# A fused Perceiver block on one core: scores of the next pair issued before the weighted sum, both row maxima behind them, and the context rows copied by VectorE

## What is computed

```python
def xattn(Q, K):                       # 16 heads, latents of width 32
    C_q, C_kv = Q @ Wq_d, K @ Wkv_d    # 512 -> 64, 512 -> 32
    CqWqk = (C_q @ W_qk).reshape(b, n, 16, 32)
    scores = einsum('bnhl,bkl->bhnk', CqWqk, C_kv) / sqrt(32)
    V_up = (C_kv @ Wv_u).reshape(b, nkv, 16, 32)
    return einsum('bhnk,bkhd->bnhd', softmax(scores), V_up)
x = x + xattn(layernorm(x), ctx)
x = x + attn(layernorm(x))             # one head of 128, Wqkv, bias, Wo, bias
xh = layernorm(x) @ hadamard           # then 4-bit codes per row, ternary weight
x = x + (codes(xh) @ ternary(weight).T)
```

## Time and profile before

| | us |
|---|---|
| time, median of 3 runs | 314.23 (314.06 to 314.25) |
| the profiled execution's own time | 315.06 |
| its span, first to last instruction | 313.3 |

### The profile page before, as it was taken

How to read it: one execution, slowest core, us unless ns; L and a number is a source line. 1 busy time by engine, 2 the same in 40 slices (tenths; PEclk the granted TensorE clock), 3 DMA queues, 4 the chain that set the end, 5 groups by cost and what they waited for, 6 DMA issues and landing times.

```text
span 313.3 us, 8324 instructions
## 1 busy us (share of the span) xinstructions
PE 299.5 (96%) x3043; PEld 207.5 (66%) x3058; DVE 246.9 (79%) x530; ACT 208.1 (66%) x587; POOL 90.0 (29%) x130
## 2 busy tenths in 40 slices
PE   7997989999999999999999999999999999999993
PEld 6754857667576766768576766768576866648642
DVE  1689798887879878887879878887879878896366
ACT  2578478768596676768596676768596777784400
POOL 2008304140323324051323324051323324141411
PEclk9999799999999999999999999999999999999998
DMA  7995002051311603041310603051311102000001
GB/s 216 376 363 187 4 8 96 19 189 31 106 49 36 186 1 134 17 157 61 108 43 33 184 0 134 17 173 44 110 43 63 26 0 69 19 35 2 33 0 67
DMA packets 20968, 26.94 MB, mean 86 GB/s; under 512 B 10704, under 2 KB 11472, under 8 KB 20944
## 3 DMA queue, kind: packets, MB, share of 16 engines
q1 hardware_dynamic: 20944, 26.62, 26.1%
HBM read 20.71 MB, written 4.19 MB: 80 GB/s over the span
## 4 chain that ended last, share of the span: by engine, by line
PE 74%; DVE 11%; ACT 6%; DMA 3%; SPq 2%; issue 2%; POOL 0%; DVEq 0%; POOLq 0%
PE ps L1009 10%; PE ps L1074 9%; PE ps L957 7%; PE ps L1132 5%; PE ps L1112 4%; PE ps L1078 4%; PE ps L1162 4%; ACT prob L385 4%; PE ps L967 3%; PE ps L1185 3%; PE ps L1156 3%; DMA bo_row<-bo 3%; PE ps L1046 3%; PE ps L1030 2%; DVE mx L614 2%
## 5 line engine op out<-in xcount | busy, mean ns | idle before, releaser
L385 ACT ACTIVATE prob<-ps,nmx,qk_scale 128x128 f32<-128x128 f32 x240 | 89.8, 469 | 34.9 <-DVE nmx L618 34.9
L1009 PE MATMUL ps<-had_s,x3t 128*128 128x512 f32 x104 | 48.2, 605 | 0.7 <-ACT x3t L379 0.7
L614 DVE TENSOR_REDUCE mx<-ps 128x8 f32<-128x1024 f32 x31 | 37.7, 1217 | 7.0 <-PE ps L1132 7.0
L334 POOL TENSOR_TENSOR qk_scale<-aux,power 128x1 f32<-128x1 f32 x16 | 9.3, 580 | 98.4 <-DVE aux L636 98.4
L623 DVE TENSOR_REDUCE sum_a<-prob 128x8 f32<-128x1024 f32 x30 | 35.8, 1210 | 0.0
L379 ACT ACTIVATE prob_t<-ps 128x512 f32<-128x512 f32 x63 | 34.8, 622 | 0.7 <-PE ps L957 0.3
L1009 PEld LDWEIGHTS ps<-had_s,x3t 128*128 128x128 f32 x104 | 18.6, 190 | 24.5 <-issue 22.7
L957 PE MATMUL ps<-ident,prob 128*128 128x128 f32 x240 | 31.8, 276 | 2.1 <-ACT prob L385 2.1
L957 PEld LDWEIGHTS ps<-ident,prob 128*128 128x128 f32 x240 | 26.6, 141 | 5.5 <-ACT prob L385 4.7
L1074 PE MATMUL ps<-x2t,wqkv_s 128*128 128x128 f32 x224 | 28.6, 281 | 0.4
L1074 PEld LDWEIGHTS ps<-x2t,wqkv_s 128*128 128x128 f32 x224 | 26.1, 192 | 2.2 <-ACT x2t L379 1.3
(11 more groups left out here) (200 smaller groups left out, 577.1 us busy)
## 6 DMA issues: line engine op xcount, KB each, us to landing
ct<-ctx_cols SPq DMA_DIRECT2D x16, 512.0 KB, 4.8
xt<-x_cols SPq DMA_DIRECT2D x16, 256.0 KB, 2.9
xr<-x_rows SPq DMA_DIRECT2D x16, 256.0 KB, 4.2
y<-res SPq DMA_DIRECT2D x15, 256.0 KB, 2.0
had_s<-hadamard SPq DMA_DIRECT2D x1, 1024.0 KB, 7.7
w_rows<-weight SPq DMA_DIRECT2D x1, 1024.0 KB, 10.7
wqkv_s<-wqkv SPq DMA_DIRECT2D x1, 768.0 KB, 8.4
wqk<-w_qk SPq DMA_DIRECT2D x2, 128.0 KB, 4.3
```

The lines of the kernel that those rows point to most:

```text
L385: last = nc.scalar.activation(prob[:, h, :], ps[:, h // 4, (h % 4) * P:(h % 4) * P + P], ACT.Exp, bias=nmx[:, h:h + 1], scale=qk_scale[:])
L614: V.tensor_reduce(mx[:, h], ps[:, 2 * half:2 * half + 2, :].rearrange("p r (c k) -> p (r c) k", c=EC), AX.X, ALU.max).then_inc(done["mx"], 1)
L1009: mm = pe.matmul(ps[:, B4, :], x3t[:, c, :], had_s[:, c, :], start=(c == 0), stop=(c == EC - 1))
```

## The change

From round 2 on (`scores_first`), and with line numbers of the kernel before:

- TensorE: `projected` (L1030) goes ahead of the second attention's scores (L1097) and now also waits for `read["qk"]`. The scores (L1132) go ahead of L1142, and the weighted sum (L1112) behind it.
- The copy of the context rows goes from ScalarE to VectorE (`context`), ahead of the second attention's maximum (L644).
- VectorE: in odd rounds the row statistics (L628 to L636) go ahead of the query copy (L640). The maximum over banks 2 and 3 leaves the next round's place behind the `x2` statistics and stands right behind the one over banks 0 and 1, ahead of `prod` (L769) and `x3` (L776). The tail loses its copy of it (L859, L862).

```diff
+        def scores_first(i, par):
+            return not (isinstance(i, int) and i <= 1)
...
# ScalarE
-                if front and not (isinstance(i, int) and i == 0):
+                if front and not scores_first(i, par) and not (isinstance(i, int) and i == 0):
                     after(act, made["ckv"], i + 1)
                     copy(ckv[:, 1 - par], ps[:, B1, 0:2 * SKV]).then_inc(read["ckv"], 1)
...
# VectorE
+                def context():
+                    after(dve, made["ckv"], i + 1)
+                    V.tensor_copy(ckv[:, 1 - par], ps[:, B1, 0:2 * SKV]).then_inc(read["ckv"], 1)
...
-                if cross and not (first and i == 1):
+                if cross and first and (i == 0 or i == 2):
                     largest(i, 1)
...
+                if front and scores_first(i, par) and par == 1:
+                    row_variance()
+                    row_scale()
                 if front and par == 1 and not alone(i) and not (first and i == 1):
                     second_query()
+                if front and scores_first(i, par):
+                    context()
                 if self_ and not (first and i == 1):
                     second_max()
                 if cross and par == 0 and not (first and i == 0):
                     sums(1)
-                if front and not (first and 0 <= i <= 1):
+                if front and not (scores_first(i, par) and par == 1) and not (first and 0 <= i <= 1):
                     row_variance()
                     row_scale()
...
                     largest(i + 1, 0)
+                    if scores_first(i, par):
+                        largest(i + 1, 1)
...
-            V.tensor_reduce(mx[:, 8:16], ps[:, 2:4, :].rearrange("p r (c k) -> p (r c) k", c=EC), AX.X, ALU.max)\
-                .then_inc(done["mx"], 1)
-            dve.wait_ge(done["mx"], N * 2 + 2)
-            V.tensor_scalar(nmx[:, 8:16], mx[:, 8:16], qk_scale[:], -1.0, ALU.mult, ALU.mult).then_inc(done["nmx"], 1)
...
# TensorE
+                if front and scores_first(i, par):
+                    after(pe, read["qk"], i - 1)
+                    after(pe, read["lat"], i + 1)
+                    projected()
...
-                if front and not (first and i == 0):
+                if front and not scores_first(i, par) and not (first and i == 0):
                     projected()
...
-                if cross:
+                if cross and not scores_first(i, par):
                     weighted_sum()
+                if front and scores_first(i, par):
+                    scores()
                 if self_:
                     after(pe, done["exp2"], i - 1, 2)
                     pe.transpose(ps[:, B3, 0:P], p2[:], ident[:]).then_inc(made["p2t"], 1)
-                if front and not (first and i == 0):
+                if cross and scores_first(i, par):
+                    weighted_sum()
+                if front and not scores_first(i, par) and not (first and i == 0):
                     scores()
```

## The result

The change makes the kernel slower: **328.07 us** (327.81 to 329.24, 4 runs) against 314.24 (314.06 to 315.74, 4 runs), a ratio of 1.0444 with a 95% interval of 1.0423 to 1.0465, or +13.8 us. The profiled execution took 328.21 us, its span is 326.4 us.

A forecast was written before the change was run, and what follows sets the result against it. TensorE, busy 96%, was taken as the bound, with VectorE's x3 just in time. Six even and six odd rounds, 6 x (1.82 + 0.56) = 14.3, plus 2.1 for round 14, gave +16.4 us: 330.6 us, range 326 to 336.

The forecast's parts named there:

- x3 had next to no slack: At the end of round 8, VectorE's x3 comes just in time: it ends at 168.87 and TensorE needs it at 168.97.
- the second maximum: On VectorE ahead of prod and x3, it costs the same 1.39 us again as the first maximum with its negative.
- Even rounds: VectorE's list sets the end, with the x3 transposes 7.98 us behind the context rows: +1.82 us a round.
- Round 14: Same distance to the x3 transposes as round 8 but no gain at the x2t copy: +2.1 us.
- Odd rounds: VectorE sets the end at 6.49 us behind the context rows against TensorE's own 6.32: +0.56 us a round.
- The earlier `x2t` copy: In even rounds, ScalarE's earlier copy ends TensorE's 0.27 us wait ahead of L1074, of which 0.25 us is gained.
- TensorE hardly stands still: In round 8's 5.64 us from the weighted sum to the x3 transposes, TensorE was said to have almost no idle time.
- The sum: Six even and six odd rounds cost 14.3 us; with round 14 and the tail, +16.4 us together.
- Scores issued early bring nothing by themselves: In even rounds the scores end long before VectorE turns to them at 3.64 us, so issuing them early brings nothing.
- TensorE's clock: Rival: the granted clock falls in the new gaps, 1.7 us lost in every even round, +12 us, 342 us; chance 0.11.
- Faster: Rival: the x3 transposes don't wait for x3, VectorE having over 1.8 us to spare: 312.5 us; chance 0.03.
- refunded: Rival: TensorE runs ahead elsewhere and takes up x3's lateness, leaving 314 to 320 us; chance 0.06.

The follow-up runs named there:

- e1: The changed kernel with the second maximum put back behind the x2 statistics of the next round, and in the tail: 319.21 us, ratio 1.0128 to the kernel before.
- e3: The kernel before with only the second maximum moved, so that both maxima stand behind the scores: 328.50 us, ratio 1.0438.
- e5: The changed kernel with even rounds laid out as odd ones, second row sums and row statistics ahead of VectorE's context copy: 321.40 us, ratio 1.0195.
- e4: The kernel before with TensorE's new order alone, ScalarE making the context copy ahead of the two exponentials: 318.09 us, ratio 1.0094.
- e8: e5 with context matmuls between two sets of transposes and, in even rounds, row statistics behind the second attention's maximum: 321.06 us, ratio 1.0186.
- e2: The changed kernel with the context copy given back to ScalarE, ahead of its two exponentials of the second attention: 328.92 us, ratio 1.0458.
- e9: e6 with, in even rounds, ScalarE also copying query and key ahead of the second copy of probabilities: 314.62 us, ratio 0.9979.
- e6: The kernel before with, in even rounds, two instead of three exponentials of the second half ahead of the x2t copy: 313.81 us, ratio 0.9978.
- e7: The changed kernel with the second maximum moved behind x3, still in the same round: 326.02 us, ratio 1.0365.

## Why the prediction was right, and where its sizes were off

The sign, the mechanism and the place in even rounds were as forecast: 330.6 was forecast, +16.4 us, and 328.07 came, +13.8. The odd rounds came out near by their number, but what sets their end was taken wrongly. Point by point:

- **x3 had next to no slack, and the second maximum is what it waits for in even rounds.** Shown by e1 and e3, and by the wait of 1.32 us ahead of L983. The second maximum took 1.39 us of VectorE's list (172.76 - 171.37), the forecast term to the digit; taking it out in e1 gave 1.22 us back in the round. "No slack" was a little too strong: before, `x3` started 0.83 us behind `prod`, where 0.66 is enough in the changed kernel, and TensorE, not VectorE's list, held it back, so the list had 0.17 us to spare.
- **Even rounds: +1.82 forecast, +1.69 measured** in rounds 6 to 10. The term was 0.13 too large. L983 starts 7.89 us behind the context matmuls where 7.98 was worked out: the maximum follows the copy's start by 0.34 instead of 0.44, and `x3` follows `prod` by 0.66 instead of 0.74, against 0.13 more between that maximum and the first row maximum (3.28 instead of 3.15). In rounds 2 and 4 the excess was 1.36 and 1.55 only. Round 14 gave 2.04, forecast 2.1.
- **Odd rounds: +0.56 forecast, +0.29 to +0.40 measured**, and this is the step that failed in its reasons. I had VectorE set the end, at 6.49 behind the context matmuls against 6.32 for TensorE. L983 of round 7 starts at 6.39. In the trace `x3` ends at 157.17, TensorE's L978 at 157.27, and L983 follows it without a wait. TensorE's own order sets the end there and in rounds 5, 9 and 11; in rounds 3 and 13 L983 does wait, 0.17 and 0.18 us, for `x3`. TensorE waited longer ahead of the scores than I took: from the copy's end (151.27) to the scores 0.29 us pass, where I had 0.06; and from the scores' start to L983 5.66 us pass, where I had 5.80. The two errors work against each other, so that the odd term came out near is in part luck.
- **The earlier `x2t` copy: 0.25 us forecast, 0.14 measured.** L1085 starts 6.26 us behind the start of round 8, and L1074 before 6.40 us. The rest is lost because the transposes of `x2n` start 0.13 us later there (4.90 us instead of 4.77).
- **A wait of before was inside a number.** The chain gives L1030 0.63 us before, yet 0.45 after. The two matmuls are the same. Before, the weight loads of the weighted sum behind them waited for the last probability copy, in 13 rounds:

```profile
PEld ps L1112 <- ACT prob_t L379: 4.7, 13, 0.7
```

I read the difference as this wait, which the chain counted into L1030; that is argued from the order, and no run tests it. By it "TensorE hardly stands still" was too strong by 0.1 to 0.2 us a round. What the trace does show is that the context matmuls of the changed kernel ended earlier than I had them (10.51 us behind the start of round 8, where 10.59 was worked out).
- **The sum.** Rounds 2 to 13 were to cost 14.3 us and cost 11.7; round 14 and the tail were to cost 2.1 and cost 2.0. Of the 2.6 us, 0.7 lie in rounds 2 and 4. The 0.83 us that was added between the median and the profiled execution did not come back: the profile before had a granted clock of 0.79 from 28 to 36 us, the one after 1.00, and it lies 0.14 us above its median.
- **Scores issued early bring nothing by themselves** was said of even rounds and was right there (they end long before VectorE turns to them). It doesn't hold for odd ones: e3 shows that without them VectorE waits 0.77 us.
- **TensorE's clock** (rival): the page's row of the granted clock stays at 9 through all slices, and the mean is 1.000 in this execution. Gaps of up to 1.5 us in the rounds and one of 1.82 us at the head of the tail were not followed by a lower clock. The three executions that were not profiled have means of 0.996, 0.997 and 0.991, and the last took 329.24 us; where they lost it isn't known, but no such loss comes near the 12 us of this rival. **Faster** and **refunded** fell too: work that came early only waited elsewhere, as the table of waits shows.

## What to carry to other kernels

When one engine is nearly always busy, ending another engine's wait that isn't on the chain need not bring anything (here 26 us of ScalarE's waiting for the maxima went and 13.8 us were lost). Before moving a step on an in-order engine, look at what is listed behind it and how much slack that has: ahead of `x3`, which was done only 0.1 us before TensorE was free for its reader, the maximum took 1.39 us of VectorE's list and 1.2 us of an even round, and in e5, with other work moved into VectorE's idle stretch, it stands in the same place and the matmuls of round 8 have no marked wait for `x3` any more. And where a matmul, the copy of its result and the matmul that uses it follow each other, TensorE needs other work in between. Taking that work away exposed the context copy (0.50 us in e4), and shifting the first matmul forward exposed the next copy (0.42 us in e8).

## What the runs showed beside that

**The same gap, with and without a lower clock.** In round 1 the order of the instructions is the same in all these kernels, and TensorE waits there for ScalarE. In e4 and e2 the windows around this gap read (busy us of the engines, then granted clock, DMA share, GB/s; e4 first):

```profile
28.00:36.00 8.00, 5.93 (x44) 5.17 (x43) 7.72 (x15) 5.87 (x14) 5.46 (x6) 0.79 0.48 163
```

```profile
28.00:36.00 8.00, 5.86 (x55) 5.10 (x54) 7.72 (x15) 6.07 (x16) 5.63 (x6) 1.00 0.43 159
```

Both had a gap of 2.07 to 2.08 us just before 31 us, with TensorE busy 5.9 of 8 us; the mean clock fell to 0.79 in one, with 0.50 in the 2 us from 32 to 34 (1.2 GHz), and stayed at 1.00 in the other. Over the eleven profiled executions: seven had the gap of 2.07 to 2.08 us, and the clock of this stretch fell in five of them (before, e1, e4, e5, e9) and not in two (e2, e8). Four had a shorter gap there, 1.47 to 1.64 us (changed, e3, e6, e7), and it fell in none.

Of the 17 runs of the kernel before that were taken beside e5 to e7, the eight with a mean clock of 0.996 or more took 313.43 to 314.25 us, the eight with 0.991 or 0.992 took 315.14 to 316.02, and one with 0.657 took 418.51. 1.3 us between the medians of the two eights is more than e6 gains; with like clocks e6 stands at 313.46 against 314.13 and at 314.98 against 315.43. But the mean clock doesn't tell all: of the 17 runs beside e8 and e9, three with 0.999 or 1.000 took 315.3 to 315.4 us and one with 0.992 took 314.31. What decides whether the clock falls these runs don't tell.

**A scaled negative beside GpSimd.** The 128x8 step behind a maximum takes 0.23 us at the round's end. In the old place of the second maximum it overlaps with GpSimd's `x2n` and takes 0.57, as in round 8 of e1. That the overlap is the cause wasn't tried.

```profile
158.38 0.77 POOL L317 TENSOR_SCALAR x2n<-x,aux,rstd 128x512 f32<-128x512 f32 x1 [0.18 <-POOL rstd L314]
```

```profile
158.61 0.57 DVE L622 TENSOR_SCALAR nmx<-mx,qk_scale 128x8 f32<-128x8 f32 x1
```

**From the context copy's end to TensorE's first score matmul** 0.14 us pass in even rounds of the changed kernel (168.17 to 168.31) and 0.29 in odd ones (151.27 to 151.56). In odd rounds the scores wait for the query copies too. In e8, where the probability copy is what they wait for last, 0.05 us pass (148.74 to 148.79). Which of the waits makes the difference was not tried.
